# Expert blocks of 128 rows set between blocks of 256 rows, instead of behind all of them

## What is computed

```python
scores = jax.nn.softmax(xf @ gate_w.T + gate_b, axis=-1)
top_w, top_idx = lax.top_k(scores, K)          # K = 2 of E = 8 experts
...
h = jax.nn.silu((xf @ gw.T + gb) * (xf @ uw.T + ub))   # F = 816
return (acc + w[:, None] * (h @ dw.T + db), None)
```

## Time and profile before

| what | value |
|---|---|
| median of 3 runs | 1111.12 us (1106.53 to 1115.45) |
| profiled execution | 1106.13 us |
| its span | 1104.3 us |
| its mean granted TensorE clock | 0.967 |

### The profile page before, as it was taken

How to read it: one execution, slowest core, us unless ns; L and a number is a source line. 1 busy time by engine, 2 the same in 40 slices (tenths; PEclk the granted TensorE clock), 3 DMA queues, 4 the chain that set the end, 5 groups by cost and what they waited for, 6 DMA issues and landing times.

```text
span 1104.3 us, 28738 instructions
## 1 busy us (share of the span) xinstructions
PE 1026.8 (93%) x8622; PEld 949.4 (86%) x8622; DVE 831.9 (75%) x1954; ACT 812.0 (74%) x1982; POOL 726.4 (66%) x1051
## 2 busy tenths in 40 slices
PE   4867989999999999989899999999999999999994
PEld 3645878787878888869899999999999999999994
DVE  6588566666666666666788888887888898886782
ACT  6545868686868686865888888887888788875673
POOL 3367656363636464533578888887888888887765
PEclk9978999999999999999999999999999999997897
DMA  9890012020111111414521222246323532366741
GB/s 309 249 305 25 26 59 72 34 66 34 60 40 52 48 38 38 165 36 148 173 61 28 35 38 38 38 111 204 74 38 90 133 71 38 101 209 181 223 127 39
DMA packets 61810, 106.39 MB, mean 96 GB/s; under 512 B 8960, under 2 KB 50688, under 8 KB 59584
## 3 DMA queue, kind: packets, MB, share of 16 engines
q1 hardware_dynamic: 47680, 86.04, 24.3%
q0 software_dynamic: 14080, 19.74, 9.4%
HBM read 128.55 MB, written 35.59 MB: 149 GB/s over the span
## 4 chain that ended last, share of the span: by engine, by line
PE 58%; DVE 10%; ACT 9%; issue 8%; DMA 8%; POOL 6%; POOLq 0%; DVEq 0%; ACTq 0%; SPq 0%
PE bank L1413 15%; PE bank L1415 15%; PE bank L1414 15%; DMA out_dram<-ys,dest 6%; POOL ht L713 3%; DVE sm L1154 3%; PE bank L1504 3%; ACT sm L812 3%; PE bank L1514 3%; PE bank L1542 2%; PE bank L1535 2%; PE bank L1710 1%; DVE wide_share L1163 1%; PE bank L1747 1%; POOL out_dram L725 1%
## 5 line engine op out<-in xcount | busy, mean ns | idle before, releaser
L1413 PE MATMUL bank<-xt_h,gu_s 128*128 128x256 f32 (+3 forms) x1014 | 291.5, 287 | 6.0 <-DVE hf L1336 5.6
L1414 PE MATMUL bank<-xt_l,gu_s 128*128 128x256 f32 (+3 forms) x1014 | 289.0, 285 | 0.0
L1415 PE MATMUL bank<-xt_h,gu_s 128*128 128x256 f32 (+3 forms) x1014 | 288.4, 284 | 0.0
L713 POOL TENSOR_TENSOR ht<-hf,ht 128x256 fp32r<-128x256 f32 (+3 forms) x273 | 234.3, 866 | 64.3 <-ACT ht L939 54.5
L1413 PEld LDWEIGHTS bank<-xt_h,gu_s 128*128 128x128 f32 (+1 forms) x1014 | 195.8, 193 | 7.1 <-issue 6.3
L1322 DVE TENSOR_TENSOR gu_s<-raw_gu,gu_s 128x512 fp32r<-128x512 f32 (+1 forms) x273 | 200.0, 754 | 1.8 <-ACT gu_s L946 1.6
L1415 PEld LDWEIGHTS bank<-xt_h,gu_s 128*128 128x128 f32 (+1 forms) x1014 | 195.7, 193 | 0.0
L1414 PEld LDWEIGHTS bank<-xt_l,gu_s 128*128 128x128 f32 (+1 forms) x1014 | 195.4, 193 | 0.0
L927 ACT ACTIVATE gs<-bank,bias 128x256 f32<-128x256 f32 (+1 forms) x234 | 105.2, 452 | 95.2 <-PE bank L1415 92.7
L725 POOL DMA_INDIRECT out_dram<-ys,dest x71 | 117.4, 1653 | 53.3 <-POOL ht L713 25.7
L812 ACT ACTIVATE sm<-sm,least 128x256 f32<-128x256 f32 x256 | 126.9, 500 | 33.6 <-DVE least L1154 33.5
(11 more groups left out here) (210 smaller groups left out, 2680.7 us busy)
## 6 DMA issues: line engine op xcount, KB each, us to landing
raw_gu<-in_gu_dram SPq DMA_DIRECT2D x39, 1648.0 KB
raw_dw<-in_dw_dram SPq DMA_DIRECT2D x39, 768.0 KB
xr<-xs_dram SPq DMA_DIRECT2D x32, 258.0 KB, 2.7
xs_dram<-zrec SPq DMA_DIRECT2D x5, 1548.0 KB, 17.6
raw_dw<-in_dw_dram SPq DMA_DIRECT2D x78, 64.0 KB
xwin<-xt_dram SPq DMA_DIRECT2D x7, 640.0 KB, 4.2
xt_dram<-xt SPq DMA_DIRECT2D x8, 512.0 KB, 5.8
xres<-in_x_dram SPq DMA_DIRECT2D x8, 512.0 KB, 3.8
```

The costliest lines, as they stand in the source:

```text
L713: nc.gpsimd.tensor_tensor(low, hf[0:m, ring(c), 0:n], ht[0:m, p, 0, c, 0:n].bitcast(F32), ALU.subtract).then_inc(h_split, 1)
L1413: nc.tensor.matmul(dst, lhs[0], rhs[0], start=start, stop=False)
L1414: nc.tensor.matmul(dst, lhs[0], rhs[1], start=False, stop=False)
L1415: return nc.tensor.matmul(dst, lhs[1], rhs[0], start=False, stop=stop)
```

## The change

The sequence of blocks becomes: 0 to 26 with 256 rows, then five pairs and two more, so that blocks 27, 29, 31, 33, 35, 37 and 38 have 128 rows and 28, 30, 32, 34 and 36 have 256. Which rows belong together, the layout of `xs_dram` and the slots of the tokens stay the same. `ROW_OF` gives the first row of a block, `constants` writes the block's number within its kind, and `route_blocks` makes three comparisons in place of two. The loops stop before block 24, 25 or 26, as each engine's loop needs, and the rest is unrolled. No wait, buffer or order inside a block is changed.

```diff
+NE = 26
+SMALLS = [*range(NE + 1, NB, 2), NB - 1]
+WHOLES = [b for b in range(NB) if b not in SMALLS]
+ROW_OF = {b: n * BT for n, b in enumerate(WHOLES)} | {b: NF * BT + n * P for n, b in enumerate(SMALLS)}
...
-    c[:, C_BLK:C_BLK + NB] = np.concatenate([np.arange(NF), np.arange(NS)])[None, :]
+    for part in (WHOLES, SMALLS):
+        c[:, [C_BLK + b for b in part]] = np.arange(len(part))[None, :]
...
-            with eng.Fori(0, (NF - 4) // 2) as i:
+            with eng.Fori(0, (NE - 4) // 2) as i:
                 body(i * 2 + 2, 0)
                 body(i * 2 + 3, 1)
-            for b in range(NF - 2, NB):
+            for b in range(NE - 2, NB):
                 body(b, b % 2)
 
         def tiles_of(b):
 
-            return 1 if isinstance(b, int) and b >= NF else 2
+            return 1 if isinstance(b, int) and b in SMALLS else 2
...
-                    sp.dma_start(xr[:, p], xs_dram[ds(b * BT, BT), :].rearrange("(t p) c -> p t c", p=P)).then_inc(xr_loaded[p], 16)
+                    sp.dma_start(xr[:, p], xs_dram[ds(ROW_OF[b] if isinstance(b, int) else b * BT, BT), :].rearrange("(t p) c -> p t c", p=P)).then_inc(xr_loaded[p], 16)
                 else:
-                    sp.dma_start(xr[:, p, 0], xs_dram[ds((b + NF) * P, P), :]).then_inc(xr_loaded[p], 16)
+                    sp.dma_start(xr[:, p, 0], xs_dram[ds(ROW_OF[b], P), :]).then_inc(xr_loaded[p], 16)
...
-                for at, end, ends in ((0, NF, r8[3]), (NF, NB, r8[10])):
-                    wide = [P, end - at, E]
-                    link(nc.vector.tensor_tensor(rb[:, at:end, :], spread(cst[:, C_BLK + at:C_BLK + end], wide), across(ends[:, :], wide), ALU.is_ge))
+                pairs = slice(NE + 1, NB)
+                for at, ends in ((slice(0, NB), r8[3]), (pairs, r8[10]), (slice(NB - 1, NB), r8[10])):
+                    count = (at.stop - at.start) // (2 if at is pairs else 1)
+                    wide = [P, count, E]
+                    ask = cst[:, C_BLK + at.start:C_BLK + at.stop]
+                    to = rb[:, at, :]
+                    if at is pairs:
+                        ask = ask.rearrange("p (n o) -> p n o", o=2)[:, :, 0]
+                        to = to.rearrange("p (n o) e -> p n o e", o=2)[:, :, 0, :]
+                    link(nc.vector.tensor_tensor(to, spread(ask, wide), across(ends[:, :], wide), ALU.is_ge))
```

More of the change, by code:

```diff
@@ L33 @@
 SLOTS = NF * BT + NS * P
+NE = 26
+SMALLS = [*range(NE + 1, NB, 2), NB - 1]
+WHOLES = [b for b in range(NB) if b not in SMALLS]
+ROW_OF = {b: n * BT for n, b in enumerate(WHOLES)} | {b: NF * BT + n * P for n, b in enumerate(SMALLS)}
+assert len(SMALLS) == NS and WHOLES[0:NE + 1] == [*range(NE + 1)]
 REC = D + 2
@@ L523, in load_block @@
                 load_bias(b, p)
-            with sp.Fori(0, (NF - 4) // 2) as i:
+            with sp.Fori(0, (NE - 4) // 2) as i:
                 load_block(i * 2 + 3, 1)
                 load_block(i * 2 + 4, 0)
-            for b in range(NF - 1, NB):
+            for b in range(NE - 1, NB):
                 load_block(b, b % 2)
@@ L746, in _ @@
                 body(b, b % 2)
-            with pool.Fori(0, (NF - 4) // 2) as i:
+            with pool.Fori(0, (NE - 4) // 2) as i:
                 body(i * 2 + 3, 1)
                 body(i * 2 + 4, 0)
-            for b in range(NF - 1, NB):
+            for b in range(NE - 1, NB):
                 body(b, b % 2)
@@ L1399, in _ @@
             body(3, 1)
-            with dve.Fori(0, (NF - 6) // 2) as i:
+            with dve.Fori(0, (NE - 6) // 2) as i:
                 body(i * 2 + 4, 0)
                 body(i * 2 + 5, 1)
-            for b in range(NF - 2, NB):
+            for b in range(NE - 2, NB):
                 body(b, b % 2)
```

## The result

| | before | after |
|---|---|---|
| median | 1111.53 us | 1129.81 us |
| lowest to highest | 1106.53 to 1115.45 | 1125.91 to 1136.73 |
| ratio of after to before | | 1.0174, 95% interval 1.0109 to 1.0239 |
| profiled execution | 1106.1 us, span 1104.3 | 1125.91 us, span 1123.1 |

The change costs 1.7%. Each ratio in this document is the recorded one of the undisturbed executions of two kernels and need not equal the quotient of the medians beside it, which in experiments 5 and 7 each include one execution at a far lower clock (0.75 and 0.84). The kernel before was run again beside every experiment (medians 1109.91 to 1112.78), and the ratios of the experiments are to these.

The account below looks back on a forecast made before the run. TensorE, busy for 93% of the span, was taken to bound the kernel. -15.4 + 5 x (1.2 + 5.6) + 1.0 + 0.3 = +19.9 us on the profiled 1106.1 gave 1126.0; forecast 1128, range 1096 to 1147.

Parts of the forecast that it names:

- Part 1: Run of seven smalls behind block 31 taken away: losses of blocks 32 and 35 given back, 7.2 + 8.2 = 15.4 us.
- what I said would show: Sign on the weight loads: no block of 27 to 38 waits for a `raw_gu`.
- Part 2: Blocks 29, 31, 33, 35, 37: TensorE waits 1.2 us for VectorE's first product before gate-up's fourth chunk; bounds 0.6, 3.3.
- Part 3: All five pauses among 128-row matmuls bring TensorE's clock down, at 5.6 us each; ends 4 and 6.5.
- Part 4: Weights for 36 and 37 both new: 1 us more on block 37's pause; `route_blocks` some 0.3 more.
- contention rival: Each pause 3.3 us, each fall 6.5, and block 27 loses 7.2: +41, 1147 us; chance 0.06.
- `route_blocks`, 0.3: Three comparison instructions for two, 0.67 us now, some 0.3 more, counted because VectorE releases TensorE there.
- the queues don't get longer: SyncE and GpSimd: same loads and scatters per block, a small needing one scatter, so no added queueing.
- The median, 2 on top: Before's median is 5.0 above its profiled execution, about one more fall; forecast put between 1126 and 1131, at 1128.
- The rival "no pause": VectorE's tail behind a whole under 4.6 us, so nothing waits in small-whole pairs: 1091 us; chance 0.17.
- The rival "the clock mostly holds": Pauses in the odd blocks, no fall 1098 us, two or three 1109 to 1115; chances 0.08 (one or none), 0.14.

Follow-up runs that it names:

- 5: Changed kernel with VectorE's casts of `gu_high` for the next block but one placed between the small block's chunks: 1120.58 us, ratio 1.0063 to before.
- 7: Changed kernel, where the next block is small: `gu_high` casts between the small's chunks and its first product ahead of the down-weight split: 1113.51 us, ratio 1.0031 to before.
- experiment 3: Changed kernel with no new weights loaded from block 27 on, computing with those in the buffers: 1120.2 us (one execution).
- experiment 4: Changed kernel with the 128-row blocks at 20, 23, 26, 29, 32, 35 and 38, each behind two wholes: 1111.16 us, ratio 1.0007 to before.
- 2: Kernel before with the next block's chunk 0 (ScalarE's bias, VectorE's product) ahead of `dw_high` and `dw_low`: 1107.35 us, ratio 0.9951 to before.
- 6: Kernel before with the `gu_high` casts moved between the small block's chunks (for blocks 31 to 36): 1109.91 us, ratio 0.9986 to before.
- 8: Kernel before, where the next block is small: `gu_high` casts between the small's chunks and its first product ahead of the down-weight split: 1113.08 us, ratio 0.9998.
- 10: Kernel before with extra VectorE casts ahead of the first product: four in block 28, seven in 30, one in 34, two in 37: 1114.28 us (one execution).
- experiment 1: Changed kernel with the next block's chunk 0 (ScalarE's bias, VectorE's product) ahead of `dw_high` and `dw_low`: 1128.81 us, ratio 1.0166 to before.
- 9: Changed kernel with 128-row blocks at 20, 23, 26, 29, 32, 35, 38 and the next block's first product ahead of `dw_high` and `dw_low`: 1104.88 us, ratio 0.9957.

## Why the prediction held, point by point

Forecast 1128 (1096 to 1147), slower with 0.58: measured 1129.81. The sum against the profiled execution gave 1126.0, and it was 1125.9. That is closer than its terms were.

- **Part 1, what is given back: 15.4.** Right: 15.9 were lost in the old order, 15.5 in the two blocks. (The clock row has three of its last four slices below 9, not two, and it hides a third fall, that of block 1, which the change leaves alone: 18.99 and 19.09.) One cast did wait for `raw_gu` (1.16, ahead of block 28), against what I said would show; it lies where the cover is long, and TensorE waited for nothing.
- **Part 2, the race: a pause of 1.2 in each odd block, none in the even ones.** Right in place and size: 1.10, 1.08, 1.10 and 1.09 in the last four. z0 came 7.48 behind the gate-up's end, predicted 7.5. Even that was two small errors against each other: z6 at 1.74 for 1.93, z6 to z0 5.74 for 5.58. Experiments 3 and 4 show the mechanism: without loads the pause stays, and with another order it goes to the block whose cover is the `down` of a small.
- **Part 3, the clock: five falls at 5.6.** The price was right, the number was not. Less their pauses, blocks 29, 31, 33 and 35 lost 6.5, 5.0, 6.4 and 5.0, 5.7 on average. But the 1.09 of block 37 brought no fall. With the 1 us on block 37, 35.0 were predicted for the odd blocks from 29 on; 9.3 + 6.1 + 7.5 + 6.1 + 1.3 = 30.3 were measured.
- **Part 4 and the contention rival.** The extra of 1 us was put on block 37, by way of a count of loads. It came in blocks 26 to 28 instead, 1.9 + 0.6 + 0.75, and in the pause of 29, 2.77. The bounds had it (z6 up to 3.0 late, a pause up to 3.3); it was a fair part of the rival called contention, in one place of five. Block 27 doesn't carry more than the later ones: 225 GB/s over 14.41 us and 166 over 19.91 in block 31 are 3.2 and 3.3 MB each; block 29 of before has 154 over 14.52, 2.2 MB. What is late there is GpSimd. In block 27 it waits for a scatter to land, which it doesn't in experiment 3, without the loads:
```profile
932.01 0.28 POOL L702 COPY dest<-kept 128x2 uint32<-128x2 uint32 x1 [2.01 <-DMA out_dram<-ys,dest]
```
  VectorE and GpSimd ahead of block 29's z0:
```profile
945.54 0.48 DVE L1349 SCALAR_TENSOR_TENSOR hf<-bank,bias,gs 128x256 f32<-128x256 f32 x1 [0.59 <-POOL ht L719]
946.05 0.49 DVE L1352 SCALAR_TENSOR_TENSOR hf<-bank,bias,gs 48x256 f32<-48x256 f32 x1
946.57 3.68 DVE L1328 CAST gu_s<-raw_gu 128x512 fp32r<-128x512 f32 x4
```
```profile
946.56 2.50 POOL L719 TENSOR_TENSOR ht<-hf,ht 128x256 fp32r<-128x256 f32 x3
949.24 0.73 POOL L719 TENSOR_TENSOR ht<-hf,ht 48x256 fp32r<-48x256 f32 x1 [0.18 <-POOL ht L719]
```
  The products wait for GpSimd's `ht`, so z6 is late (3.17 for 1.74), and those `ht` then run beside nearly the whole of the four casts: 3.68 for 2.69. The Trainium skill (Perfetto Trace Analysis, Optimizing Scalar/DVE Operations) says that GpSimd and VectorE share a read port of SBUF, and that these casts are held up by GpSimd's work fits it; no run here takes the port by itself.
- **`route_blocks`, 0.3.** The comparisons take 0.85 for 0.63 us, 0.2. That "the queues don't get longer" missed the end, where one scatter more costs 1.0 us.
- **The median, 2 on top.** I put the 5.0 us between before's profiled execution and its median down to "about one more fall". No run shows that. In the five traces with the front of before (before, 2, 6, 8, 10) the expert stage starts between 520.2 and 525.5 us, and before's is the earliest, so such a spread lies ahead of all blocks. That the median came out at 1129.8 for 1128 is no evidence for the term.
- **The rival "no pause"** (1091, by the interleaving of busy stretches). Refuted: an undisturbed pair would take 13.83 + 11.90 = 25.7, no pair reached it, and block 30 shows VectorE with 4 us idle while block 31 waits for it. Averages over a pair don't help an engine that works in order against two buffers.
- **The rival "the clock mostly holds"** was right in one block of five.

So the mechanism was right, and that the sum came out to 0.1 us is luck: one fall too many and the 1 us on block 37 stand against the losses of blocks 26 to 29, the slower last block (1.0) and 1.0 more outside the span (2.8 for 1.8).

What stays open: what tells the 1.09 of block 37, and the 1.08 of two blocks in experiment 3, from equal pauses that bring a fall. Block 37 has a fall in experiments 1 and 3 and none in after, behind 0.99, 1.08 and 1.09, so it is neither the block nor the length. Nor was it settled whether the load burst of blocks 17 to 19 in experiment 4 can be spread.

## What to carry to other kernels

When pieces of work of two sizes alternate, count for each place what the in-order engines must finish and what cover the bottleneck engine has until it needs it: the cover is set by the neighbours (here the `down` of the block before the last), and the average over a pair hides it. Put the short piece where the piece that follows its cover is itself long, as in experiment 4; there a pause cost little more than its length, while among 128-row matmuls it cost five to seven times that where the clock fell (6.1 us for 1.10, 7.5 for 1.08). That makes mixing cheap and didn't make it pay: experiment 4 is no faster than before. And take moves of single instructions for what they are in an engine without spare time: the work moved back comes again as a delay of the next deadline, or uncovers the next wait (ScalarE in 5, the load of rows in 7).

## What the runs showed of the hardware

- The same pause brings TensorE from 2.4 to 1.2 GHz or not. Among 128-row matmuls, pauses of 0.98 to 1.16 us in front of the fourth chunk did it in 13 of 16 blocks: 3 of 4 in after (31 to 37), 4 of 4 in experiment 1, 3 of 5 in 3, 2 of 2 in 6 and 1 of 1 in 10. 0.69 (before), 0.85 and 0.86 did it, and so did each of the five from 1.63 to 2.77; 0.47 (twice) and 0.60 did not. In front of the transposes 0.79 and 0.49 did (blocks 31 and 35 of experiment 7), 0.51 did not (block 29). Among 256-row matmuls of a gate-up, pauses up to 2.45 did not: 0.96 (four times), 1.19 and 2.45 in experiment 4, 0.92 in 5, 0.98 in 7, 1.85 in 10, 1.55 in block 1 of 1, 2 and 9, 1.47 and 1.48 in two other blocks of 9. The 2.7 of block 1 did, in all nine traces that have it, for 3.4 us. Two pauses of 0.75 to 0.91 within 1.4 us of each other in the `down` of a whole brought a fall of 3.4 us three times (block 19 of 4, block 26 of 5 and 7) and none in block 31 of 8 (0.77 and 0.75) or block 16 of before (1.02 and 0.76).
- Among 128-row matmuls a fall cost mostly 4.8 to 6.5 us beside the pause; the ends are 3.3 (block 34 of experiment 2) and 8.0 (block 34 of 10). In blocks 29 to 35 of after the clock came back during the `down` that followed.
- Four casts of 128x512 on VectorE took 2.69 us with GpSimd's `ht` beside them for 1.9 us (block 31 of after), and 3.68 with it beside them for 3.2 (block 29).
